# Splitting the squares of the queries into two rounded products, one pipeline step later

## The reference

```
x = x + xattn(layernorm(x), ctx, Wq, Wk, Wv, Wo, gq, gk)

q = (hidden @ Wq).reshape(B, Sq, H, D)          # 16 heads of 128
k = (encoder @ Wk).reshape(B, Skv, H, D)
q = q * rsqrt(mean(q**2, -1) + 1e-5) * gq        # RMS norm over D = 128
k = rmsnorm(k, gk)
scores = q . k * scale;  softmax;  out = attn @ v @ Wo
```

## Time and profile before

| | us |
|---|---|
| median of 3 runs | 1527.63 (1527.08 to 1528.84) |
| the profiled execution | 1526.53 |
| its span, first to last instruction | 1524.8 |
| first matmul of item 0 | 22.94 |
| last instruction of the stage | 136.04 |
| first work of the second stage on PE | 139.14 |

### The profile page before, as it was taken

One profiled execution on the slowest core, in us unless ns is written; L12 is line 12 of the kernel. 1 busy time (PEld: TensorE's weight loads), 2 busy tenths in 40 slices (PEclk: granted clock), 3 DMA queues, 4 the chain that ended last, 5 costly groups with the idle time before them and its releaser, 6 DMA issues. The chain is left out here.

```text
span 1524.8 us, 29153 instructions
## 1 busy us (share of the span) xinstructions
PE 1438.0 (94%) x6176; PEld 973.3 (64%) x6176; DVE 1300.6 (85%) x2093; ACT 1156.1 (76%) x4810; POOL 942.6 (62%) x1474
## 2 busy tenths in 40 slices
PE   5996999999999999999999999999999999976886
PEld 3664666666666666666666666666666666853554
DVE  6876888998988898889888998988998988765985
ACT  5886888787888887788878787887878877534763
POOL 4001778887878887788878787878887876010000
PEclk9998999999999999999999999999999999996998
DMA  3000000000000000000000000000001011000000
GB/s 139 37 1 1 1 1 23 7 17 17 8 22 2 23 1 22 2 22 1 22 2 22 10 13 21 3 22 2 23 1 47 1 49 42 1 1 0 8 7 15
DMA packets 9818, 25.05 MB, mean 16 GB/s; under 512 B 736, under 2 KB 6016, under 8 KB 9520
## 3 DMA queue, kind: packets, MB, share of 16 engines
q1 hardware_dynamic: 9648, 23.49, 4.3%
HBM read 22.44 MB, written 1.05 MB: 15 GB/s over the span
## 5 line engine op out<-in xcount | busy, mean ns | idle before, releaser
L807 PE MATMUL psK<-wkh,c_cTh 128*124 128x512 f32 x832 | 509.2, 612 | 6.1 <-DVE c_prod L1235 2.8
L1235 DVE TENSOR_TENSOR c_prod<-psK,c_c 124x512 f32<-124x512 f32 x624 | 427.0, 684 | 65.6 <-PE psK L807 61.7
L1529 POOL TENSOR_TENSOR c_acc<-c_acc,c_prob 123x1024 f32<-123x1024 f32 (+1 forms) x192 | 459.1, 2391 | 2.6 <-issue 1.4
L827 PE MATMUL psO<-c_prob,raw 123*128 123x512 f32 (+1 forms) x832 | 424.9, 591 | 0.0
L1021 ACT ACTIVATE c_unused<-c_prod 124x128 f32<-124x128 f32 x832 | 247.5, 299 | 110.5 <-DVE c_prod L1235 110.5
L1252 DVE TENSOR_TENSOR c_prob<-psS,c_ss 124x512 f32<-124x512 f32 x416 | 286.9, 690 | 50.2 <-PE psS L818 34.8
L807 PE MATMUL psK<-wkl,c_cTh 128*124 128x512 f32 x832 | 328.6, 395 | 0.0
L1027 ACT ACTIVATE c_prob<-c_prob,shift 124x1024 f32<-124x1024 f32 x208 | 238.9, 1149 | 56.7 <-DVE c_prob L1252 45.4
L1242 DVE TENSOR_REDUCE c_ss<-c_prod 124x8 f32<-124x1024 f32 x208 | 253.8, 1220 | 7.2
L1013 ACT ACTIVATE c_unused<-psK 124x128 f32<-124x128 f32 x832 | 218.8, 277 | 52.9 <-PE psK L807 37.4
L807 PEld LDWEIGHTS psK<-wkh,c_cTh 128*124 128x124 f32 x832 | 154.4, 186 | 143.6 <-issue 88.7
(11 more groups left out here) (312 smaller groups left out, 2311.5 us busy)
## 6 DMA issues: line engine op xcount, KB each, us to landing
raw<-in_ctx SPq DMA_DIRECT2D x16, 799.5 KB
raw<-in_L_xattn_Wq SPq DMA_DIRECT2D x3, 512.0 KB, 9.7
xs<-in_x SPq DMA_DIRECT2D x1, 1024.0 KB, 5.7
big<-in_L_xattn_Wk SPq DMA_DIRECT2D x1, 1024.0 KB, 9.0
c_prod<-in_L_xattn_Wo SPq DMA_DIRECT2D x1, 1024.0 KB, 5.2
out<-s_y SPq DMA_DIRECT2D x8, 128.0 KB, 1.7
big<-in_L_ffn_W_qkv SPq DMA_DIRECT2D x1, 768.0 KB, 12.9
c_wqkv<-in_L_attn_W_qkv SPq DMA_DIRECT2D x1, 768.0 KB, 15.9
```

The lines of the kernel that those rows point to most:

```text
L807: last = nc.tensor.matmul(psK[0:ROWS, c % 2, :], x[:, slot, :], w[:, cols], start=(n == 0), stop=(n == len(terms) - 1))
L827: nc.tensor.matmul(psO[:, half, :], raw[0:rows, b, tile, :], prob[0:rows, probs(v), half * BANK:(half + 1) * BANK], start=(tile == 0), sto ...
L1235: nc.vector.tensor_tensor(prod[:, k % 2, c - GRAM, :].rearrange("p (h c) -> p h c", c=CD), psK[0:ROWS, c % 2, :].rearrange("p (h c) -> p h ...
L1529: nc.gpsimd.tensor_tensor(acc[0:rows, batch % 2, :], acc[0:rows, batch % 2, :], prob[0:rows, probs(s), :], ALU.add).then_inc(S.acc, 1)
```

## The change

The sum of squares is no longer one plain float32 product. GpSimd makes a high part `squareh` (a rounding copy, written as an addition of a column of zeros, `blank`) and a low part `squarel` of every square. PE multiplies both by `onesr`, the ones in float32r. The sum and the logarithm belong now to item o, so they come one step later. On ACT the logarithm stands first in a step; on DVE `qgl` stands before the operations of item o, and `scaled` is gone: its result is written over `half`. ACT therefore waits for `root` of the item before, where it waited for `newton`, before it writes `half`.

`squarel` shares its memory with `square`. The last quarter of `Wq` is loaded into a free part of `T.queries` instead of a tile of its own, and each quarter is loaded by two DMAs instead of one. GpSimd makes only the first low part of `Wq`; DVE makes the other three in steps 3, 9 and 17. GpSimd fills `raw` with zeros in four parts, behind items 20 to 23.

GpSimd's part of the new loop, with `ZERO_AT = (20, 21, 22, 23)` and `ZERO` the four quarters of `raw`:

```diff
+            nc.gpsimd.memset(blank[:, :], 0.0).then_inc(S.blank, 1)
...
+            def step(n, m, o):
+                if m is None:
+                    return
+                pool.wait_ge(S.square, m + 1)
+                if m >= 2:
+                    pool.wait_ge(S.total, m - 1)
+                nc.gpsimd.tensor_tensor(squareh[:, m % 2, :], square[:, m % 2, :], blank[:, :].broadcast_to([P, BANK]), ALU.add).then_inc(S.squareh, 1)
+                pool.wait_ge(S.squareh, m + 1)
+                nc.gpsimd.tensor_tensor(squarel[:, m % 2, :], square[:, m % 2, :], squareh[:, m % 2, :].bitcast(F32), ALU.subtract).then_inc(S.squarel, 1)
+                if m in ZERO_AT:
+                    if m == ZERO_AT[0]:
+                        pool.wait_ge(S.wql, KC - 1)
+                    nc.gpsimd.memset(T.raw[:, ZERO[ZERO_AT.index(m)]], 0.0).then_inc(S.zeroed, 1)
```

TensorE, behind `psK` of item n:

```diff
-                if m is not None:
-                    pe.wait_ge(S.square, m + 1)
-                    if m >= 2:
-                        pe.wait_ge(S.newton, m - 1)
-                    nc.tensor.matmul(psS[:, m % 2, :], T.ones[:, :], square[:, m % 2, :], start=True, stop=True).then_inc(S.total, 1)
                 if o is not None:
+                    if o == 0:
+                        pe.wait_ge(S.onesr, 1)
+                    pe.wait_ge(S.squarel, o + 1)
+                    if o >= 2:
+                        pe.wait_ge(S.newton, o - 1)
+                    nc.tensor.matmul(psS[:, o % 2, :], onesr[:, :], squareh[:, o % 2, :], start=True, stop=False)
+                    nc.tensor.matmul(psS[:, o % 2, :], onesr[:, :], squarel[:, o % 2, :], start=False, stop=True).then_inc(S.total, 1)
                     pe.wait_ge(S.qgl, o + 1)
```

ScalarE, the waits and the logarithm:

```diff
             def step(n, m, o):
+                if o is not None:
+                    act.wait_ge(S.total, o + 1)
+                    nc.scalar.activation(log[:, :], psS[:, o % 2, :], ACT.Ln, scale=1.0 / D, bias=T.eps[:, :]).then_inc(S.log, 1)
                 if n is not None:
                     act.wait_ge(S.q, n + 1)
                     if n >= 2:
-                        act.wait_ge(S.total, n - 1)
+                        act.wait_ge(S.squarel, n - 1)
...
                     if o:
-                        act.wait_ge(S.newton, o)
+                        act.wait_ge(S.root, o)
                     nc.scalar.activation(half[:, :], y[:, o % 2, :], ACT.Square, scale=float(np.sqrt(0.5 / D))).then_inc(S.half, 1)
-                if m is not None:
-                    act.wait_ge(S.total, m + 1)
-                    nc.scalar.activation(log[:, :], psS[:, m % 2, :], ACT.Ln, scale=1.0 / D, bias=T.eps[:, :]).then_inc(S.log, 1)
```

VectorE, with `LOW_Q_AT = (3, 9, 17)`:

```diff
+                if n is not None:
+                    if n in LOW_Q_AT:
+                        q = LOW_Q_AT.index(n) + 1
+                        dve.wait_ge(S.wqh, q + 1)
+                        nc.vector.tensor_tensor(halved(wql[:, :, quad(q)]), wq(q), halved(wqh[:, :, quad(q)]).bitcast(F32), ALU.subtract).then_inc(S.wql, 1)
+                    dve.wait_ge(S.qgh, n + 1)
+                    nc.vector.scalar_tensor_tensor(qgl[:, n % Q_SLOTS, :], psK[:, n % 2, :], T.gcol[:, 1:2], qgh[:, n % Q_SLOTS, :].bitcast(F32),
+                                                   ALU.mult, ALU.subtract).then_inc(S.qgl, 1)
                 if o is not None:
                     dve.wait_ge(S.half, o + 1)
                     if o:
                         dve.wait_ge(S.root, o)
-                    nc.vector.scalar_tensor_tensor(scaled[:, :], psS[:, o % 2, :], float(D * EPS), half[:, :], ALU.add, ALU.mult).then_inc(S.newton, 1)
...
+                    nc.vector.scalar_tensor_tensor(half[:, :], psS[:, o % 2, :], float(D * EPS), half[:, :], ALU.add, ALU.mult).then_inc(S.newton, 1)
                     dve.wait_ge(S.newton, o + 1)
-                    nc.vector.scalar_tensor_tensor(root[:, :], scaled[:, :], 1.5, y[:, o % 2, :], ALU.subtract, ALU.mult).then_inc(S.root, 1)
+                    nc.vector.scalar_tensor_tensor(root[:, :], half[:, :], 1.5, y[:, o % 2, :], ALU.subtract, ALU.mult).then_inc(S.root, 1)
```

More of the change, by code:

```diff
@@ L188 @@
 PREP_SEMS = ("x gains wk wq0 wq1 wq2 wq3 consts gprod made stats moments centred lnT lnTh lnTl wkT wkTh wkTl wqh wql "
-             "wkh wkl gram gramh graml zeroed context m8 m2 sel causal iota selb wgate wqkv turn turned gT gtop gall")
+             "wql0 onesr blank wkh wkl gram gramh graml zeroed context m8 m2 sel causal iota selb wgate wqkv turn turned gT gtop gall")
 Q_SLOTS = 3
 X_SLOTS = 2 * BANK // DIM
-ITEM_SEMS = "q square qgh qgl total log y half newton root qw out"
+ITEM_SEMS = "q square squareh squarel qgh qgl total log y half newton root qw out"
 def queries(nc, T, psum, dram):
@@ L212, in queries @@
         xTh, xTl = sb("xTh", [P, WC, NPAIR * P], F32R), sb("xTl", [P, WC, NPAIR * P], F32R)
-        square, log, half = sb("square", [P, 2, BANK]), sb("log", [P, BANK]), sb("half", [P, BANK])
-        y, scaled, root = sb("y", [P, 2, BANK]), sb("scaled", [P, BANK]), sb("root", [P, BANK])
+        with ExitStack() as shared:
+            square = shared.enter_context(nc.sbuf_tensor("q_square", [P, 2, BANK], F32))
+        squarel = sb("squarel", [P, 2, BANK], F32R)
+        squareh, onesr, blank = sb("squareh", [P, 2, BANK], F32R), sb("onesr", [P, P], F32R), sb("blank", [P, 1])
+        log, half = sb("log", [P, BANK]), sb("half", [P, BANK])
+        y, root = sb("y", [P, 2, BANK]), sb("root", [P, BANK])
         qgh, qgl = sb("qgh", [P, Q_SLOTS, BANK], F32R), sb("qgl", [P, Q_SLOTS, BANK], F32R)
@@ L232, in wq, with halved @@
             size = WC * BANK
-            return wq_last[:, :, :] if q == KC - 1 else T.raw[:, q * size:(q + 1) * size].rearrange("p (k n) -> p k n", k=WC)
+            return wq_last if q == KC - 1 else halved(T.raw[:, q * size:(q + 1) * size].rearrange("p (k n) -> p k n", k=WC))
+        def halved(x):
+            return x.rearrange("p k (m n) -> p k m n", m=2)
         def gram_bank(q):
@@ L252, in queries @@
         GAIN_AT, GAIN_ALL_AT = 28, 30
+        LOW_Q_AT = (3, 9, 17)
+        ZERO_AT = (20, 21, 22, 23)
+        ZERO = [slice(2 * NT * CD * n // 4, 2 * NT * CD * (n + 1) // 4) for n in range(4)]
         def out(n):
@@ L266, in _ @@
             for q, sem in enumerate(wq_there):
-                sp.dma_start(wq(q), dram["L0_xattn_Wq"].rearrange("(k p) n -> p k n", p=P)[:, :, quad(q)]).then_inc(sem, 16)
+                for k in range(WC):
+                    sp.dma_start(wq(q)[:, k, :, :], halved(dram["L0_xattn_Wq"].rearrange("(k p) n -> p k n", p=P)[:, :, quad(q)])[:, k, :, :]).then_inc(sem, 16)
                 if q == 0:
@@ L273, in _ @@
             sp.dma_start(wgate, dram["L0_ffn_W_gate"]).then_inc(S.wgate, 16)
-            sp.wait_ge(S.zeroed, 1)
+            sp.wait_ge(S.zeroed, len(ZERO))
             for b in range(2):
@@ L314, in _ @@
                                     ALU.subtract).then_inc(S.wkl, 1)
-            pool.wait_ge(S.wql, KC)
-            nc.gpsimd.memset(T.raw[:, :], 0.0).then_inc(S.zeroed, 1)
+            pool.wait_ge(S.blank, 1)
+            def step(n, m, o):
[11 more added lines that the diff above has]
+                    nc.gpsimd.memset(T.raw[:, ZERO[ZERO_AT.index(m)]], 0.0).then_inc(S.zeroed, 1)
+            steps(step)
         @block.tensor
@@ L385, in step @@
                     h, g = items[n]
-                    if h % HB == 0 and g == 0:
-                        pe.wait_ge(S.wql, h // HB + 1)
+                    if h == 0 and g == 0:
+                        pe.wait_ge(S.wql0, 1)
+                    elif h % HB == 0 and g == 0:
+                        pe.wait_ge(S.wql, h // HB)
                     if n >= 2:
@@ L455, in _ @@
             act.wait_ge(S.made, 1)
+            nc.scalar.activation(onesr[:, :], T.ones[:, :], ACT.Copy).then_inc(S.onesr, 1)
             def step(n, m, o):
+                if o is not None:
+                    act.wait_ge(S.total, o + 1)
+                    nc.scalar.activation(log[:, :], psS[:, o % 2, :], ACT.Ln, scale=1.0 / D, bias=T.eps[:, :]).then_inc(S.log, 1)
                 if n is not None:
```

18 lines of the change are left out of this document (7 added, 11 removed).

## The result

| | median us | ratio to before, 95% interval |
|---|---|---|
| before, 7 runs on the same chip | 1528.40 (1526.41 to 1530.23) | |
| after, 7 runs | 1534.36 (1532.47 to 1536.22) | 1.0040 [1.0028, 1.0052] |

The changed kernel is 0.4% slower, 6.0 us. The profiled execution took 1534.89 us with a span of 1533.2 us, against 1526.53 and 1524.8 before. One execution of the last experiment took 2450.31 us at a granted clock of 0.56; it is in that experiment's median, which is 1528.25 without it, and not in its ratio.

A forecast was written before the change was run, and what follows sets the result against it. The prediction took PE to bound the stage, busy 97.88 of 100 us. Ends +0.5, the 29 steps -0.3 and -0.1 gave +0.1 us; put on before's median, 1527.8 us, range 1522.5 to 1534.

The forecast's parts named there:

- the term for step 30: PE waits there for DVE's maximum, now behind three operations instead of two after `qgl`: +2.6 us.
- PE saves 0.43 a step: On PE, two rounded products (0.47 us) replace the plain one (0.90); ACT needs 2.69 and DVE 2.71 a step.
- shut each other out on `root`: `root` reads two SBUF tensors, so it and GpSimd's two operations form one queue: 2.79 us a step in good order.
- Bad steps of 3.37: Steps where `root` is asked for just after a high part begins and `half` waits for it: 3.37 us each.
- The subtractions: 8.2: DVE's weight subtractions in steps 3, 9 and 17 each turn the order bad: 2.6, 2.5 and 3.1 us.
- Gram steps 4.4: Steps 8, 12 and 16, with 12 narrow matmuls before `psK`: +1.54, +1.54 and +1.27 us.
- copies 2.3: ACT's extra copies, each of a square's size, in six steps at +0.38 us.
- square 2 at 29.35: At the stage's start, the first logarithm and square 2 stand behind a whole sum: 29.35 instead of 28.85, +0.5 us.
- the context at 130.6: The context's load, moved behind item 23's fill, lands at 130.6 us, hidden by 5 us before the stage's end.
- nothing is shut out: Rival: `root` and GpSimd do not block each other, step 2.71 us, 5 us faster, 1522.6 us; 20%.
- The bad order stays: Rival: `root` stays late behind the high part and `half` waits, 3.37 us a step, 1535.0 us; 23%.
- the order was good again: Good order is high part, low part, `root`, 2.79 us a step; gram steps and ACT's lateness restore it.

The follow-up runs named there:

- the last experiment: The kernel before with only the spread of the maximum over the gains at item 31 instead of 30: 1528.64 us, ratio 1.0004.
- the first three experiments: Edits of the kernel after: Newton result written into PSUM, 1526.93 us; `half` no longer waiting for `root`, 1530.15 us; GpSimd's pair replaced by four fills, 1522.04 us.
- the experiment with the subtractions ahead: The kernel after with DVE's three weight subtractions all ahead of item 0's `qgl`, not in steps 3, 9 and 17: 1524.28 us, ratio 0.9970.
- its variant: The kernel before with only the spread of the gains' maximum at item 31 instead of 30: 1528.64 us, ratio 1.0004.
- best: The kernel after with Newton result in PSUM, maximum's spread at item 31, and subtractions at items 1, 2 and 3: 1517.96 us, ratio 0.9940.
- the first two experiments: Edits of the kernel after: Newton result written into PSUM, 1526.93 us; `half` no longer waiting for `root`, which still reads two SBUF tensors, 1530.15 us.
- the one with fills: The kernel after with GpSimd's high and low parts replaced by four fills of ones per item: 1522.04 us, one run.
- the experiment with the spread at 31: The kernel after with the two narrow matmuls of the gains' maximum in step 31 instead of 30: 1528.90 us, ratio 1.0005.

## Why the prediction was wrong

The mechanism in the loop was right, and so was most of the sum. The step that failed is the term for step 30: the prediction priced PE's pause at +2.6 us and put what follows a pause, matmuls at the low clock, at nothing. In the profiled pair the forecast was some 8 us short: 2.9 from that term, 0.8 from the other steps, 0.8 at the start and 3.7 outside the stage. Point by point:

- *PE saves 0.43 a step, ACT and DVE then set the pace at 2.7.* Right: the quiet steps are 2.66 us (3, 4, 10, 14, 23, 25) in after.
- *GpSimd and DVE shut each other out on `root`, and `half` makes it last.* Right as to the shut-out, as the first three experiments show; of the lateness `half` carries on only a part. Bad steps of 3.37 were 3.46. The Trainium skill ("SBUF — State Buffer", section "SBUF: two separate sides") calls the shared port pair an exclusive lock. The traces agree: `root` with two SBUF inputs ended 0.56 us after the high part (37.22 + 1.40), and with one it did not wait. The high part reads a broadcast column as its second operand, and `root` waited for it all the same, which was open.
- *The subtractions: 8.2.* Measured 9.2.
- *Gram steps 4.4, copies 2.3.* Without late steps (the experiment with the subtractions ahead) steps 8, 12 and 16 are 4.15, 4.17 and 4.15, 4.1 above three of 2.79. The steps with copies are 2.98 to 3.14.
- *The start: square 2 at 29.35, 0.5 later.* After had 30.15. From the first matmul of item 0 to square 2 it took 5.91 us in before (22.94 to 28.85) and 6.44 to 6.45 in the three first experiments, which kept the full clock: +0.5, as forecast. After itself took 7.06, with the low clock from 24.0 to 27.4 us: another 0.6. The kernel before can have that too (its variant took 6.88, from 22.67 to 29.55). The first matmul began 0.15 later. So some 0.8 of the profiled difference is not shown to belong to the change.
- *The end 9.0, the context at 130.6, a stage end near 136.* 8.97, 131.1, and 140.73.
- *"In step 30 PE waits for the maximum ..., +2.6."* **This step failed.** The wait itself was forecast well (5.39 us for the step; 5.17 and 5.26 in two executions that kept the full clock). Left out was what the pause does to PE's clock. It brought step 30 to 7.24 and step 31 to 3.70, 2.9 us over the forecast. That is 2.9 of the 3.7 us missing over the 29 steps; the rest are tenths, most of them in the late steps. The rows gave no price for it, since PE in the loop of before never stood for as long as 1 us up to the last square. But the prediction named no bound for it either, and so the range ended too low.
- *Outside the stage* it expected nothing. In the profiled pair 3.7 us arose there, by the medians 1.3. Of the 3.7, 1.1 arose in the second stage (between the table loads of ACT at 138.96 and 1366.14 before, 143.66 and 1371.92 after) and 2.6 behind it, where before took 158.66 us and after 161.28. Over the twelve traces that last part, the same code in all, took 157.35 us at a granted clock of 0.86 to 162.24 at 0.83, so the 2.6 can be the execution. What is left is open. Stage end and median move together to within about 2 us in the experiments (best: 8.4 earlier, 10.3 faster).

Of the rivals, "nothing is shut out" fell by the durations of `root`. "The bad order stays" gave 1535.0, next to the measured time, but not by its mechanism: after the three subtractions three, one and two steps were late, and then the order was good again, as forecast. A time alone would have proved the wrong story here.

What stays open is when the clock falls. After the same pause of 1.93 to 1.97 us before step 30 it had fallen before the pause ended in after (and where the subtractions came first), fell 1.3 to 1.5 us behind it in the first two experiments (step 30: 6.02 and 6.05), and not at all in the one with fills. The pauses at the subtractions are as uneven. In the loops of all twelve traces there are 16 pauses of 1.9 us or more, and 12 of them were followed by the low clock, for 3.4 to 6.8 us. Behind the eight of 0.95 to 1.74 us it did not fall. With one profile each this can be the execution as well as the kernel.

## What to carry to other kernels

Before moving element-wise work to an idle GpSimd, list every VectorE operation beside it that reads two SBUF tensors, and give the recurring one an operand in PSUM: here that was worth 0.5%. One-off work of this kind belongs where no loop runs at its pace yet (0.7% for the three subtractions). A pause of TensorE is priced by its length and by the matmuls behind it at the low clock, and an idle term in a forecast needs that second bound.

## What was unexpected in the hardware

- After a pause of about 2 us in an otherwise busy loop, PE mostly ran at the 1.2 GHz level for 3.4 to 6.8 us (matmuls 0.43 us apart instead of 0.24): 12 times of 16. Before step 30 this cost 2.9 us over the forecast; over steps 19 and 20 nothing that can be seen (8.87 us with it in after, 8.85 without it in the experiment with the spread at 31).
- GpSimd's fills (0.53 us for 128x512) ran beside a VectorE operation with two SBUF inputs and delayed neither: 21 times with `root` at 0.69 us, three with a subtraction at 1.22.
- Writing the first operation's result back to PSUM in place costs next to nothing: 0.68 to 0.70 us against 0.67 to 0.69 into SBUF, and the next, reading PSUM, 0.69 again.
- The same start can get either clock level in different executions. From the first matmul to square 2 that was 1.0 us (5.91 against 6.88) with no change in this part of the code.
